# Hybrid attention and gated-unit layer on one core: finer jobs, one-operand VectorE forms, eight transposed-probability buffers, and a new hand-written order

## The chip, the cores and the metric

The kernel runs on one core of a Trainium2 chip. The metric is device time in microseconds (us), median of several runs. All engines of the core take part: TensorE (PE; its weight loads are PEld), VectorE (DVE), ScalarE (ACT), GpSimd (POOL) and SyncE (SP), which issues most DMAs.

## The reference

An input x of 8 blocks of 256 rows by 128 columns passes four stages, each added to x. LN is a LayerNorm with epsilon 1e-5.

```python
# A: attention without softmax, weights from a time difference
Q, K, V = sigmoid(4*(batchnorm(LN(x) @ W) - 1))           # for q, k, v
d = (1 - Q.mean(-1)) - (1 - K.mean(-1)).T                 # 256 x 256
x = x + (where(d < 0, f, -f) + 0.9) @ V @ Wo + bo         # f = 0.9*exp(-|d|/0.5)
# F: gated unit, hidden width 384, int weights / 127
x = x + (silu(LN(x) @ wg.T) * (LN(x) @ wu.T)) @ wd.T
# B: causal softmax attention, 16 heads of 64
x = x + attention(LN(x))
# P: the gated unit again, same weights as F
x = x + (silu(LN(x) @ wg.T) * (LN(x) @ wu.T)) @ wd.T
```

All is float32; products of float32 accuracy are built from a rounded high part (hi) and the rest (lo).

## The kernel before, in words

x stays in SBUF, with 128 rows to a partition dimension and two halves per block. Weights and x are loaded once at the start; block b's result is stored when dbP.b has been added.

There is no loop over the work. Each engine has a hand-written list of jobs, `ORDER`, and issues its jobs strictly in that order; a job is a name and a number, as `aout.3`. For the stages A, F and P and for projections of v the number is the block (0 to 7); for a pair of heads it is 8 x block + pair (0 to 63). Jobs meet by semaphores. The eight PSUM banks are shared by all: `BANKS` says which bank a job's result goes to, and `take` makes TensorE wait until the bank's last user has been read (`freed`), `full` makes a reader wait until TensorE has written. A change of an order therefore changes which job each bank waits for, too.

Jobs of one block, in the order in which they depend on each other:

- `lns` (VectorE: bn_stats, bn_aggr, then var = variance + epsilon, line 707; GpSimd: rstd by a power, line 863, and xn, line 874; in block 0 and for P.7 xn is on VectorE, line 717). The three come in one job of VectorE and one of GpSimd.
- `lnt` (TensorE transposes xn, ScalarE writes hi at line 576, VectorE lo at line 776). A, F, B and P at its end name the stage.
- Stage A: `qkv0..2` (TensorE, then tanh on ScalarE, line 587), `mean` (TensorE line 386, then VectorE: tq and ntk out of the bank, then less from tq, ntk and a zero mask, line 739), `dist` (ScalarE: |d| and exp), `sign` (VectorE line 795, both operands in SBUF), `stdp` (GpSimd line 909), `sv` (GpSimd), `vwo`, `aout` (TensorE line 404; VectorE adds to x, line 751; GpSimd's `lnsA` has put the bias in xb before).
- Stages F and P: `gF0..2` and `gP0..2`, one for each third of the hidden width (TensorE; ScalarE tanh; VectorE two operations, lines 787 and 788), then `hh` (ScalarE: hi of all three thirds in one instruction of 128x768, line 619), `hl` (GpSimd: lo, 128x768, line 903), `dn` (TensorE line 424, ScalarE), `db` (TensorE line 441 or 435, VectorE adds to x, line 755).
- Stage B, for each of 64 pairs: `qk` (TensorE; VectorE line 832 adds the bias), `scores` (TensorE lines 503 and 506), `mask` (VectorE lines 805 and 807: mask and row maximum; four instructions), `exp0`, `exp1` (ScalarE lines 645 and 647), `inverse` (VectorE line 822), `norm` (GpSimd line 916, two instructions of 128x256), `transposes` (TensorE line 518), `pt0` (ScalarE line 655) and `pt1` (VectorE line 815) into prob_t, and for two pairs at once `sum` (TensorE line 541, ScalarE). `v0..v3` give the values, `out0`, `out1` the projection (TensorE line 469, VectorE line 762); `pre0`, `pre1` start the last block's projection with six of eight pairs.
- `hot` is four transposes of the identity (lines 454 to 456) whose result nobody reads. `w0..w5` split the projection weights wqkv into hi (ScalarE line 611) and lo (GpSimd line 896, 128x512 each). `bo` adds a bias.

Buffers: three for qk, two for masked scores, four for prob, four for prob_t.

Of the kernel before, what the change touches and what calls it, by code (L numbers as in the profile page):

```python
# [39 lines left out]
W_SCALE = 1.0 / 127.0  # L40
SCORE_SCALE = A ** -0.5
# [12 lines left out]
        lntB.1 aout.2 lntA.3 v3.1 qk.8 qk.9 qk.10 qk.11 transposes.4 transposes.5 scores.8 scores.9 sum.5 transposes.6
        transposes.7 v2.1 v1.1 lntF.2 sum.7 scores.10 scores.11 gF1.2 qkv1.3 gF2.2 gF0.2 qk.12 qk.13 out0.0 v0.1 transposes.8
        transposes.9 scores.12 scores.13 out1.0 dnF.2 qkv2.3 qk.14 qk.15 qkv0.3 dbF.2 sum.9 transposes.10 transposes.11
        transposes.12 transposes.13 mean.3 vwo.3 lntB.2 scores.14 scores.15 sum.11 v3.2 lntP.0 qk.16 qk.17 aout.3 v2.2 scores.16
        scores.17 sum.13 qk.18 lntF.3 gP2.0 qk.19 v0.2 v1.2 transposes.14 transposes.15 scores.18 scores.19 transposes.16 sum.15
        transposes.17 gF1.3 gF0.3 gF2.3 qk.20 qk.21 lntA.4 qk.22 out1.1 scores.20 scores.21 gP0.0 gP1.0 out0.1 dnF.3 qkv1.4
        qkv0.4 qkv2.4 dbF.3 sum.17 transposes.18 scores.22 transposes.19 mean.4 qk.23 lntB.3 sum.19 transposes.20 transposes.21  # L60
        qk.24 qk.25 lntP.1 vwo.4 scores.23 scores.24 scores.25 qk.26 v0.3 gP2.1 lntA.5 aout.4 sum.21 transposes.22 transposes.23
        qk.27 gP0.1 dnP.0 qk.28 scores.26 scores.27 transposes.24 lntF.4 qkv2.5 v2.3 qk.29 v1.3 qkv1.5 gF0.4 gP1.1 gF1.4 gF2.4
        qkv0.5 scores.28 transposes.25 sum.23 sum.25 qk.30 qk.31 dnF.4 out0.2 dbF.4 mean.5 transposes.26 scores.29 transposes.27
        out1.2 lntB.4 vwo.5 v3.3 scores.30 scores.31 aout.5 qk.32 qk.33 dbP.0 lntP.2 dnP.1 v2.4 sum.27 transposes.28
        transposes.29 scores.32 scores.33 transposes.30 v1.4 lntA.6 lntF.5 qk.34 qk.35 dbP.1 gF1.5 gF2.5 v0.4 sum.29 scores.34
        scores.35 transposes.31 gF0.5 qkv0.6 qkv1.6 qk.36 qk.37 sum.31 transposes.32 transposes.33 gP2.2 out0.3 v3.4 dnF.5
        scores.36 scores.37 qkv2.6 dbF.5 gP0.2 qk.38 qk.39 vwo.6 mean.6 gP1.2 out1.3 lntB.5 transposes.34 transposes.35 sum.33
        sum.35 scores.38 scores.39 transposes.36 transposes.37 qk.40 qk.41 aout.6 dnP.2 v2.5 scores.40 scores.41 lntP.3 qk.42
        v1.5 v0.5 gP0.3 qk.43 lntF.6 sum.37 transposes.38 transposes.39 gF0.6 dbP.2 gF1.6 gF2.6 sum.39 scores.42 scores.43
        transposes.40 transposes.41 lntA.7 qk.44 qk.45 dnF.6 out0.4 qkv1.7 dbF.6 qkv2.7 qkv0.7 scores.44 scores.45 gP2.3 qk.46  # L70
        mean.7 lntB.6 gP1.3 out1.4 qk.47 vwo.7 sum.41 transposes.42 transposes.43 transposes.44 scores.46 scores.47
        transposes.45 sum.43 lntP.4 qk.48 qk.49 qk.50 dnP.3 aout.7 v3.5 scores.48 scores.49 transposes.46 sum.45 transposes.47
        v2.6 gP1.4 qk.51 lntF.7 gP2.4 dbP.3 gP0.4 sum.47 scores.50 scores.51 gF0.7 v1.6 gF2.7 qk.52 qk.53 gF1.7 out1.5 out0.5
        transposes.48 transposes.49 scores.52 scores.53 transposes.50 v0.6 dnF.7 qk.54 qk.55 dnP.4 dbF.7 transposes.51 scores.54
        scores.55 sum.49 sum.51 lntB.7 dbP.4 v3.6 lntP.5 qk.56 qk.57 qk.58 v2.7 transposes.52 transposes.53 scores.56 scores.57
        transposes.54 gP0.5 qk.59 qk.60 transposes.55 scores.58 scores.59 sum.53 sum.55 gP2.5 v0.7 out1.6 qk.61 v1.7
        transposes.56 transposes.57 scores.60 scores.61 transposes.58 qk.62 qk.63 out0.6 v3.7 scores.62 transposes.59 scores.63
        transposes.60 transposes.61 sum.57 lntP.6 gP1.5 sum.59 sum.61 transposes.62 transposes.63 pre0.0 gP2.6 gP1.6 sum.63
# [880 lines left out]
```

## Time and profile before

| what | value |
|---|---|
| median of 3 runs | 334.7 us (333.91 to 335.21) |
| the profiled execution's own time | 336.41 us |
| its span, first to last instruction | 334.6 us |
| granted TensorE clock | 0.998 |
| PE, PEld | 316.2, 272.4 us |
| DVE, ACT, POOL | 271.7, 245.3, 225.6 us |

The span is 1.8 us shorter than the profiled execution's time. Times of the views are counted from the span's start. Matmuls are pipelined: the durations of single matmuls overlap, so one matmul's step is better seen in the chain, where overlapping pieces are counted once.

### The profile page before, as it was taken

To read this page: it belongs to the slowest core of one execution; us is meant where nothing else is said; L and a number is where in the kernel's file an instruction comes from. 1 tells how busy PE (TensorE), PEld (TensorE's weight loads), DVE (VectorE), ACT (ScalarE), POOL (GpSimd) and SP (SyncE) were. 2 spreads that over 40 slices of the span, in tenths; PEclk is the share of its full clock that TensorE was granted. 3 is DMA by queue.
4 is the path that set the end of the run, shared out by engine and by line. 5 is a ranking of instruction groups with operands and counts; after the bars stand their busy time and mean duration, and the time that the engine had idled before them with its cause. 6 is when DMAs were issued, how large, how long until landed. Compare 5 with 4: busy or idle time off the path is not lost.

```text
span 334.6 us, 9995 instructions
## 1 busy us (share of the span) xinstructions
PE 316.2 (95%) x3216; PEld 272.4 (81%) x3216; DVE 271.7 (81%) x1092; ACT 245.3 (73%) x812; POOL 225.6 (67%) x279
## 2 busy tenths in 40 slices
PE   1998998999999999999999999999999999999995
PEld 1788886879978987898878887889888988888874
DVE  4547899868799999988998879978997988879454
ACT  2626497988779777887777876977967786698821
POOL 4437986747868879656889476863993398457630
PEclk9999999999999999999999999999999999999999
DMA  6900000000000000000001000000000000000001
GB/s 189 306 1 3 2 2 3 2 1 3 2 0 4 2 2 1 3 2 3 0 9 29 2 1 3 0 18 3 3 2 5 14 2 17 4 2 3 2 0 49
DMA packets 6419, 5.84 MB, mean 17 GB/s; under 512 B 864, under 2 KB 5856, under 8 KB 6368
## 3 DMA queue, kind: packets, MB, share of 16 engines
q1 hardware_dynamic: 6080, 4.99, 5.0%
q8 instruction: 27, 0.44, 0.5%
q10 hardware_dynamic: 288, 0.20, 0.2%
q14 instruction: 24, 0.20, 0.2%
HBM read 4.15 MB, written 1.05 MB: 16 GB/s over the span
## 4 chain that ended last, share of the span: by engine, by line
PE 77%; DVE 8%; issue 6%; POOL 4%; ACT 2%; DMA 1%; DVEq 0%; ACTq 0%; POOLq 0%
PE bank L541 12%; PE bank L355 8%; PE bank L518 7%; PE bank L506 7%; PE bank L357 6%; PE bank L356 6%; PE bank L469 6%; PE bank L503 5%; PE bank L415 4%; PE bank L416 3%; PE bank L424 2%; PE bank L373 2%; PE bank L404 2%; POOL prob L916 1%; PE bank L396 1%
## 5 line engine op out<-in xcount | busy, mean ns | idle before, releaser
L916 POOL TENSOR_TENSOR prob<-prob,row_inv 128x256 f32<-128x256 f32 (+1 forms) x128 | 103.0, 832 | 50.0 <-DVE row_inv L822 49.7
L647 ACT ACTIVATE prob<-neg_s,neg_max 128x256 f32<-128x256 f32 x128 | 63.9, 499 | 0.0
L645 ACT ACTIVATE prob<-neg_s,neg_max 128x128 f32<-128x128 f32 x128 | 50.8, 397 | 13.1 <-DVE neg_max L807 12.8
L807 DVE CUSTOM_DVE_ANT_0 neg_s<-bank,mask 128x256 f32<-128x256 f32 x128 | 53.5, 418 | 0.0
L541 PE MATMUL bank<-prob_t,v 128*64 128x256 f32 (+1 forms) x512 | 47.4, 331 | 0.0
L832 DVE TENSOR_TENSOR qk<-bank,bqk 128x512 f32<-128x512 f32 x64 | 42.7, 683 | 3.9 <-PE bank L357 3.7
L541 PEld LDWEIGHTS bank<-prob_t,v 128*64 128x64 f32 x512 | 32.1, 136 | 13.6 <-issue 2.9
L805 DVE CUSTOM_DVE_ANT_0 neg_s<-bank,mask 128x128 f32<-128x128 f32 x128 | 36.3, 284 | 4.6 <-PE bank L506 4.3
L506 PE MATMUL bank<-qk 64*128 64x256 f32 x256 | 38.5, 377 | 0.0
L355 PE MATMUL bank<-rt_hi,wqkv_hi 128*128 128x256 f32 x128 | 38.1, 298 | 0.4 <-DVE rt_lo L776 0.4
L815 DVE COPY prob_t<-bank 128x384 f32<-128x384 f32 x64 | 33.4, 548 | 4.3 <-PE bank L518 4.1
L518 PEld LDWEIGHTS bank<-ident,prob 64*128 64x128 f32 x768 | 28.9, 139 | 8.8 <-issue 4.9
L357 PE MATMUL bank<-rt_lo,wqkv_hi 128*128 128x256 f32 x128 | 35.8, 280 | 0.0
L356 PE MATMUL bank<-rt_hi,wqkv_lo 128*128 128x256 f32 x128 | 35.8, 280 | 0.0
L655 ACT ACTIVATE prob_t<-bank 128x384 f32<-128x384 f32 x64 | 29.3, 485 | 8.6 <-PE bank L518 8.4
L518 PE MATMUL bank<-ident,prob 64*128 64x64 f32 x768 | 32.7, 226 | 1.8 <-DVE qk L832 0.8
L469 PE MATMUL bank<-wo,zt 128*128 128x128 f32 x232 | 28.4, 276 | 0.0
L503 PE MATMUL bank<-qk 64*128 64x128 f32 x256 | 27.9, 295 | 0.0
L469 PEld LDWEIGHTS bank<-wo,zt 128*128 128x128 f32 x232 | 27.1, 192 | 0.5 <-issue 0.3
L503 PEld LDWEIGHTS bank<-qk 64*128 64x128 f32 x256 | 21.8, 187 | 6.4 <-issue 3.1
L355 PEld LDWEIGHTS bank<-rt_hi,wqkv_hi 128*128 128x128 f32 x128 | 24.1, 188 | 2.2 <-issue 0.8
L645 ACT ACTIVATION_READ_ACCUMULATOR prob<-neg_s,neg_max 128x1 f32 x128 | 24.8, 193 | 0.0
(162 smaller groups left out, 831.1 us busy)
## 6 DMA issues: line engine op xcount, KB each, us to landing
wqkv<-wqkv_in SPq DMA_DIRECT2D x3, 512.0 KB, 7.4
x<-x_in SPq DMA_DIRECT2D x8, 128.0 KB, 6.0
out<-x SPq DMA_DIRECT2D x8, 128.0 KB, 1.8
wo<-wo_in SPq DMA_DIRECT2D x1, 512.0 KB, 7.0
wa<-wa_in ACTq DMA_DIRECT2D x1, 192.0 KB, 3.0
wg_i<-wg_in SPq DMA_DIRECT2D x1, 192.0 KB, 3.2
wu_i<-wu_in SPq DMA_DIRECT2D x1, 192.0 KB, 3.4
wd_i<-wd_in SPq DMA_DIRECT2D x1, 192.0 KB, 4.4
```

The costliest lines, as they stand in the source:

```text
L355: nc.tensor.matmul(out, w_hi_ap, r_hi_ap, start=True, stop=False)
L356: nc.tensor.matmul(out, w_lo_ap, r_hi_ap, start=False, stop=False)
L357: return nc.tensor.matmul(out, w_hi_ap, r_lo_ap, start=False, stop=True)
L469: last = nc.tensor.matmul(out[:, 0:D], zt[:, b % 2, u, j * P:(j + 1) * P], wo[:, u, :], start=(u == 0), stop=(u == U - 1))
L503: nc.tensor.matmul(home(f"s{e}", m)[0][:, 0:P], qk[half, r, 0, 0:P], qk[half, r, 1, 0:P], start=True, stop=True)
L506: nc.tensor.matmul(S[:, P:SC], qk[half, r, 0, P:N], qk[half, r, 1, :], start=True, stop=True).then_inc(done, 1)
L518: last = nc.tensor.transpose(out[:, at:at + A], prob[half, m % 4, e, j * P:(j + 1) * P], ident[half, half])
L541: last = nc.tensor.matmul(out[half, t + k * P:t + N], v[:, b % 2, k, h * A:(h + 1) * A], prob_t[:, i % 4, e, cols], start=(k == 0), stop=( ...
L645: nc.scalar.activation(prob[:, r, e, 0:P], neg_s[:, m % 2, e, 0:P], ACT.Exp, bias=neg_max[:, q, 2 * e:2 * e + 1], scale=-1.0, accum_out=ro ...
L647: nc.scalar.activation(prob[:, r, e, P:SC], neg_s[:, m % 2, e, P:SC], ACT.Exp, bias=neg_max[:, q, 2 * e + 1:2 * e + 2], scale=-1.0, accum_ ...
L807: nc.vector.tensor_tensor_reduce(out=neg_s[:, m % 2, e, P:SC], in0=S[:, P:SC], in1=mask[:], scale=-SCORE_SCALE, scalar=3e38, op0=ALU.add, ...
L916: nc.gpsimd.tensor_tensor(pr, pr, inv, ALU.mult).then_inc(p_norm, 1)
```

## The change

1. *Epsilon.* bn_aggr now writes to `mv_eps`, three numbers per half: mean, variance and a constant EPS set once by a memset. var is a tensor_reduce that adds the last two.
2. *Comparison from PSUM.* ntk = -(k + 0.5) becomes tk = k + 0.5, and less is a tensor_scalar that reads the bank and compares with tk; the bank is freed after it. dist waits for a semaphore of its own, mean_s, and is abs(tk - tq) by a scale of -1.
3. *Gated units by chunk.* hh and hl become three jobs each, of 128x256.
4. *Eight buffers of prob_t*, four of them in the space of wqkv, which is read for the last time when all six weight parts are split.
5. *Finer jobs.* What VectorE's and GpSimd's first `lnsA` held of the A stage's constants becomes `ga` and `gb`, the VectorE xn becomes `xnA.0`, `xnF.0`, `xnB.0`, `xnP.7`, the casts of the gated unit's weights `wf`, the bias of stage A `xb`. Three of the six lo parts of wqkv (`w0`, `w2`, `w4`) are VectorE's.
6. *New lists and banks* for all engines; 18 `hot` jobs, 16 before.

```diff
-        last = nc.vector.bn_aggr(mv[c][:, j, :], stats[c][:, j, :])
+        last = nc.vector.bn_aggr(mv[c][:, j, 0:2], stats[c][:, j, :])
     link(last)
-    nc.vector.scalar_tensor_tensor(var[c][:], mv[c][:, :, 1], EPS, mv[c][:, :, 1], ALU.add, ALU.max).then_inc(var_s[k], 1)
+    nc.vector.tensor_reduce(out=var[c][:], in_=mv[c][:, :, 1:3], axis=mybir.AxisListType.X, op=ALU.add).then_inc(var_s[k], 1)
...
     nc.vector.tensor_scalar(tq[:, b % 2, :], src[:, 0:N], 0.5, None, ALU.add)
-    nc.vector.tensor_scalar(ntk[:, b % 2, :], src[:, N:N + T], 0.5, -1.0, ALU.add, ALU.mult).then_inc(free, 1)
+    nc.vector.tensor_scalar(tk[:, b % 2, :], src[:, N:N + T], 0.5, None, ALU.add).then_inc(mean_s, 1)
...
     for j in range(T):
-        last = nc.vector.scalar_tensor_tensor(less[:, j, :].rearrange("p (k s) -> p k s", s=P), tq[:, b % 2, :].rearrange("p (k s) -> p k s", s=P),
-                                              ntk[:, b % 2, j:j + 1], mask[:, 0:P].unsqueeze(1).to_broadcast([P, T, P]), ALU.add, ALU.is_lt)
-    last.then_inc(less_s, 1)
+        last = nc.vector.tensor_scalar(less[:, j, :], src[:, 0:N], 0.5, tk[:, b % 2, j:j + 1], ALU.add, ALU.is_lt)
+    last.then_inc(free, 1)
...
-    nc.scalar.activation(hid_hi[k][:], hid[k][:], ACT.Copy).then_inc(hh_s[k], 1)
+    nc.scalar.activation(hid_hi[k][:, c, :], hid[k][:, c, :], ACT.Copy).then_inc(hh_s[k][c], 1)
...
-    nc.gpsimd.tensor_tensor(hid_lo[k][:], hid[k][:], hid_hi[k][:].bitcast(F32), ALU.subtract).then_inc(hl_s[k], 1)
+    nc.gpsimd.tensor_tensor(hid_lo[k][:, c, :], hid[k][:, c, :], hid_hi[k][:, c, :].bitcast(F32), ALU.subtract).then_inc(hl_s[k][c], 1)
...
+elif job[0] == "w":                       # VectorE: w0, w2, w4
+    i = int(job[1])
+    dve.wait_ge(w_hi[i], 1)
+    ws = slice(i % 2 * HALF, (i % 2 + 1) * HALF)
+    nc.vector.tensor_tensor(wqkv_lo[:, i // 2, ws], wqkv[:, i // 2, ws], wqkv_hi[:, i // 2, ws].bitcast(F32), ALU.subtract).then_inc(w_lo[i], 1)
...
+def weights_split(eng, m):                # called by both evacuations into prob_t
+    if m == PT_BUFS // 2:
+        for i in range(6):
+            eng.wait_ge(w_lo[i], 1)
```

The start of the lists, as far as the prediction speaks of it:

```diff
 PE
-lntA.0 hot.0 qkv1.0 qkv0.0 qkv2.0 mean.0 vwo.0 lntA.1 hot.1 hot.2 hot.3 qkv0.1 aout.0 qkv1.1 hot.4 hot.5 mean.1 qkv2.1
-lntF.0 hot.6 hot.7 gF2.0 gF0.0 gF1.0 bo.0 lntA.2 dbF.0 qkv2.2 vwo.1 hot.8 qkv1.2 qkv0.2 hot.9 lntB.0 aout.1 qk.0 qk.1
+hot.0 hot.1 hot.2 hot.3 hot.4 lntA.0 hot.5 qkv0.0 qkv1.0 qkv2.0 mean.0 lntA.1 hot.6 hot.7 qkv0.1 qkv1.1 vwo.0 hot.8
+aout.0 mean.1 hot.9 hot.10 lntF.0 qkv2.1 hot.11 gF0.0 gF2.0 gF1.0 lntA.2 bo.0 dbF.0 qkv2.2 hot.12 vwo.1 vwo.2 qkv0.2
+qkv1.2 lntB.0 aout.1 qk.0 qk.1 v3.0 scores.0 scores.1
...
+lntB.1 aout.2 lntA.3 qk.8 qk.9
 DVE
-lnsA.0 lntA.0 lnsA.1 mean.0 sign.0 lntA.1 lnsA.2 aout.0 lnsF.0 bv.0 lntF.0 mean.1 gF2.0 gF0.0 gF1.0 lntA.2 sign.1 dbF.0
-lnsB.0 lnsA.3 lntB.0 bo.0 aout.1
+lnsA.0 ga.0 xnA.0 lnsA.1 lntA.0 gb.0 mean.0 lntA.1 sign.0 wf.0 w4.0 aout.0 lnsF.0 lnsA.2 xnF.0 mean.1 lntF.0 bv.0 gF0.0
+gF2.0 gF1.0 w2.0 lntA.2 sign.1 bo.0 dbF.0 lnsB.0 w0.0 xnB.0 lnsA.3 lntB.0 aout.1
 ACT
-lntA.0 qkv1.0 qkv0.0 qkv2.0 w3.0 w2.0 dist.0 lntA.1 w4.0 vwo.0 qkv0.1 qkv1.1 qkv2.1
+lntA.0 qkv0.0 qkv1.0 w0.0 qkv2.0 lntA.1 dist.0 w4.0 vwo.0 qkv0.1 w3.0 qkv1.1
```

and their end:

```diff
 PE
-... sum.59 sum.61 transposes.62 transposes.63 pre0.0 gP2.6 gP1.6 sum.63
-gP0.6 pre1.0 out0.7 out1.7 dnP.5 hot.10 hot.11 hot.12 lntP.7 hot.13 hot.14 gP2.7 gP0.7 gP1.7 dbP.5 dnP.6 hot.15 dbP.6 dbP.7
+... transposes.61 transposes.62 transposes.63 sum.61 sum.63
+lntP.6 pre0.0 gP2.6 out0.7 pre1.0 out1.7 gP1.6 dnP.5 gP0.6 hot.13 hot.14 lntP.7 hot.15 hot.16 gP2.7 gP0.7 gP1.7 dnP.6
+dbP.5 hot.17 dbP.6 dbP.7
 DVE
-lntP.6 gP1.5 pt1.62 pt1.63 gP2.6 gP1.6 gP0.6 out0.7 out1.7 lnsP.7 lntP.7 gP2.7 gP0.7 gP1.7 dbP.5 dbP.6 dbP.7
+lntP.6 out0.7 gP2.6 out1.7 lnsP.7 gP1.6 xnP.7 gP0.6 lntP.7 gP2.7 gP0.7 gP1.7 dbP.5 dbP.6 dbP.7
```

## Rows read from the trace of the kernel before

**Rows 1.** The page: busy time of each engine, its share of the span, instructions.
```profile
PE 316.2 (95%) x3216; PEld 272.4 (81%) x3216; DVE 271.7 (81%) x1092; ACT 245.3 (73%) x812; POOL 225.6 (67%) x279
```

**Rows 2.** Chain that ended last, 0 to 36 us: start us, us, what.
```profile
10.84 1.22 PE bank L386 x2
...
12.07 0.65 PE bank L388 x4
...
18.58 1.29 PE bank L404 x8
...
28.91 1.31 DVE signed L795
...
34.74 0.39 PE bank L355
```

**Rows 3.** Timeline, 14 to 36 us: start us, us, instruction [idle before <-releaser].
```profile
15.74 0.62 POOL L909 TENSOR_SCALAR stdp<-signed 128x512 f32<-128x512 f32 x1 [2.85 <-DVE signed L795]
...
19.90 0.42 DVE L751 TENSOR_TENSOR x<-bank,xb 128x256 f32<-128x256 f32 x1 [3.05 <-PE bank L404]
...
21.44 0.60 PE L386 MATMUL bank<-t_qkv,mean_w 128*128 128x256 f32 x2
...
24.03 1.96 POOL L874 TENSOR_SCALAR xn_A<-x,mv_A,rstd_A 128x128 f32<-128x128 f32 x2
...
24.60 0.89 DVE L739 SCALAR_TENSOR_TENSOR less<-tq,ntk,mask 128x256 f32<-128x256 f32 x2
...
30.58 0.49 DVE L700 BATCH_NORM_STATS2 stats_B<-x 128x6 f32<-128x128 f32 x2
```

**Rows 4.** Timeline around the longest hole on TensorE, 48 to 53 us.
```profile
48.32 2.87 DVE L739 SCALAR_TENSOR_TENSOR less<-tq,ntk,mask 128x256 f32<-128x256 f32 x2
...
48.89 2.01 POOL L903 TENSOR_TENSOR hid_lo_F<-hid_F,hid_hi_F 128x768 fp32r<-128x768 f32 x1
...
52.44 0.59 PE L424 MATMUL bank<-hid_hi_F,wd 128*128 128x256 f32 x3 [1.54 <-DVE neg_max L807]
```

**Rows 5.** Timeline, three more holes on TensorE (129 to 276 us).
```profile
131.44 0.59 PE L518 MATMUL bank<-ident,prob 64*128 64x64 f32 x12 [0.77 <-DVE qk L832]
...
208.68 0.53 PE L518 MATMUL bank<-ident,prob 64*128 64x64 f32 x10 [0.56 <-issue]
...
275.27 0.41 PE L441 MATMUL bank<-ident,dnt_F 128*128 128x128 f32 x2 [0.45 <-DVE qk L832]
```

**Rows 6.** Costs by line: instruction xcount | busy us, mean ns | idle before.
```profile
L707 DVE SCALAR_TENSOR_TENSOR var_P<-mv_P 128x2 f32<-128x2 f32 x7 | 4.4, 634 | 0.2
...
L707 DVE SCALAR_TENSOR_TENSOR var_A<-mv_A 128x2 f32<-128x2 f32 x8 | 3.1, 382 | 0.3
...
L739 DVE SCALAR_TENSOR_TENSOR less<-tq,ntk,mask 128x256 f32<-128x256 f32 x16 | 10.7, 711 | 0.3
...
L733 DVE TENSOR_SCALAR tq<-bank 128x256 f32<-128x256 f32 x8 | 3.3, 414 | 3.5 <-PE bank L388 3.5
...
L896 POOL TENSOR_TENSOR wqkv_lo<-wqkv,wqkv_hi 128x512 fp32r<-128x512 f32 x6 | 7.6, 1282 | 0.7 <-DVE xn_B L717 0.7
...
L619 ACT ACTIVATE hid_hi_F<-hid_F 128x768 fp32r<-128x768 f32 x7 | 5.9, 848 | 2.5 <-DVE hid_F L788 2.4
...
L903 POOL TENSOR_TENSOR hid_lo_F<-hid_F,hid_hi_F 128x768 fp32r<-128x768 f32 x7 | 13.0, 1856 | 4.9 <-ACT hid_hi_F L619 4.9
...
L744 DVE CAST wg<-wg_i 128x384 fp32r<-128x384 int32 x1 | 0.4, 353 | 0.0
```

**Rows 7.** Line 707: duration ns min/median/max, first and last start.
```profile
L707 DVE SCALAR_TENSOR_TENSOR var_P<-mv_P x7: 161/775/953, 92.7 to 306.0; 128x2 f32<-128x2 f32 x7
```

**Rows 8.** Chain that ended last, 320 to 326 us: start us, us, what.
```profile
320.40 0.89 PE bank L469 x8
...
324.19 0.45 PE bank L373 x2
...
325.55 0.39 PE bank L415
```

More of the change, by code:

```diff
@@ L54 @@
[L54 to L78, printed above, removed]
@@ new lines @@
+        aout.3 lntP.0 v3.2 scores.16 scores.17 sum.13 qk.18 qk.19 lntF.3 gP2.0 v2.2 v1.2 v0.2 transposes.14 transposes.15
+        scores.18 scores.19 transposes.16 transposes.17 sum.15 gF1.3 gP1.0 gF2.3 gF0.3 lntA.5 qkv2.4 out1.1 qk.20 qkv0.4 qk.21
+        qk.22 scores.20 scores.21 dnF.3 out0.1 dbF.3 gP0.0 transposes.18 scores.22 transposes.19 sum.17 qkv1.4 qk.23 lntB.3
+        vwo.4 mean.4 qk.24 qk.25 sum.19 transposes.20 transposes.21 scores.23 scores.24 scores.25 sum.21 qkv2.5 aout.4 lntP.1
@@ new lines @@
+        v0.3 qk.26 qk.27 gP2.1 dnP.0 transposes.22 transposes.23 scores.26 scores.27 transposes.24 v1.3 lntF.4 qk.28 qk.29
+        lntA.6 qk.30 qkv1.5 gF1.4 gP1.1 qkv0.5 gF0.4 gF2.4 v2.3 vwo.5 gP0.1 qk.31 scores.28 transposes.25 sum.23 sum.25 dbP.0
+        dnF.4 mean.5 dbF.4 out1.2 transposes.26 transposes.27 scores.29 scores.30 scores.31 out0.2 lntB.4 aout.5 dnP.1 v2.4
+        qk.32 qk.33 v3.3 qkv2.6 sum.27 transposes.28 transposes.29 scores.32 scores.33 transposes.30 lntF.5 v0.4 qk.34 v1.4
@@ new lines @@
+        gF1.5 qkv1.6 qk.35 gF0.5 gF2.5 scores.34 scores.35 transposes.31 sum.29 qk.36 vwo.6 qk.37 lntP.2 dbP.1 transposes.32
+        scores.36 scores.37 transposes.33 sum.31 gP1.2 gP2.2 dnF.5 out1.3 dbF.5 qkv0.6 qk.38 v3.4 qk.39 mean.6 gP0.2 out0.3
+        lntB.5 lntA.7 transposes.34 transposes.35 sum.33 sum.35 transposes.36 scores.38 scores.39 transposes.37 qk.40 aout.6
+        v0.5 v2.5 lntP.3 qk.41 qkv2.7 scores.40 scores.41 qkv0.7 gP0.3 lntF.6 dnP.2 v1.5 qk.42 dbP.2 gF2.6 qk.43 gF1.6 gF0.6
@@ L81 @@
+        scores.63 transposes.59 transposes.60 gP1.5 v3.7 sum.57 sum.59 transposes.61 transposes.62 transposes.63 sum.61 sum.63
+        lntP.6 pre0.0 gP2.6 out0.7 pre1.0 out1.7 gP1.6 dnP.5 gP0.6 hot.13 hot.14 lntP.7 hot.15 hot.16 gP2.7 gP0.7 gP1.7 dnP.6
+        dbP.5 hot.17 dbP.6 dbP.7
     """,
     "ACT": """
[L83 to L84 removed]
```

390 lines of the change are left out of this document (208 added, 182 removed).

## The prediction

> **What bounds the kernel now.** I read the page's first part, the chain of waits of the start, the timeline of the start, the costs by line, and last the timeline around the holes on TensorE. TensorE has work for 316.2 us, 95% of the span, VectorE 81% [rows 1]. From about 35 us on TensorE is the bound, and VectorE is the engine that hands it its banks. So time can come from three places: the start, where a serial chain runs until qk.0 begins at 34.74 us [rows 2]; the holes between 35 and 320 us; and the end, where the last block runs alone.
>
> The start is slow for two reasons. TensorE works at 1.2 GHz at first: mean.0 takes 1.22 + 0.65 us on the chain [rows 2], while the two matmul records of the same line L386 in mean.1 take 0.60 us at 21.44 [rows 3]. The granted clock of the run is 0.998, which hides it, so the level has to be read from the durations; the halving lies inside aout.0, which started in a nearly unbroken run of transposes. And aout.0 runs late: stdp.0 is written by 15.74 + 0.62 = 16.36 us, but aout.0's work ends on the chain at 18.58 + 1.29 = 19.87 us, and the x of block 0 is there at 19.90 + 0.42 = 20.32 us [rows 2, 3].
>
> The holes have one author. A VectorE instruction with two SBUF inputs does not run while GpSimd runs a tensor operation: less at 48.32 takes 2.87 us for two instructions while GpSimd's 768-wide hid_lo runs from 48.89 to 50.90, mask stands behind it in VectorE's order, and TensorE waits 1.54 us for that mask's bank [rows 4]. The others are 0.77, 0.56 and 0.45 us, behind less or var in the same way [rows 5]. The sum is 3.3 us. The same in the costs by line: var_P takes 634 ns for 128x2, var_A 382 ns, less 711 ns against 414 ns of tq, which reads one operand from PSUM [rows 6].
>
> **The change part by part.**
>
> *Start, up to x of block 0.* Five hot jobs (20 transposes) stand ahead of lntA.0. They need ident alone, ready near 2 us, and at a cold step of about 0.21 us end near 6.4 us, just before the first LayerNorm result (lntA.0 began at 6.68 us; it isn't held up). TensorE should then be at 2.4 GHz well before 19 us; I take before 9 us. VectorE runs lnsA.1 (about 1 us, half of it the two statistics, as in stats_B [rows 3]) before lntA.0, but the four small gb operations behind it, so qkv0.0 can start near 8.1 us; t_qkv waits for gb until about 9.35 us. mean.0 then starts near 10.5 (10.84 before) and takes 0.8 us in place of 1.87 [rows 2], ending near 11.3 us. From mean.0's end to stdp.0's took 16.36 - 12.72 = 3.6 us [rows 2, 3]; with lntA.1 put in on both ScalarE and VectorE I take 4.1, so stdp.0 is there at about 15.4 us. wf.0 and w4.0 (three casts of 0.35 and 0.8 us) now stand between sign.0 and aout.0 on VectorE and cover the 0.9 us of the matmuls with some to spare: x of block 0 near 16.8 us, 3.5 us earlier. At a still cold TensorE the gain is 1.5 us, and if aout.0 were to wait for vwo.0, which stands behind w4's copy on ScalarE, 3.0.
>
> *Start, from there to qk.0.* Before, this took 34.74 - 20.32 = 14.4 us. Three things are added on VectorE: mean.1 goes between xnF.0 and lntF.0 (1.4 us in a gap of 1.0: +0.5); w2.0 and bo.0 go ahead of dbF.0 beside sign.1, which took 1.31 us there [rows 2] (+0.4); w0.0 fills the wait for rstd_B. The last is the place where a rule speaks against the change. What the trace shows: GpSimd is held up by VectorE too; its two xn_A operations at 24.03 take 1.96 us beside less at 24.60 [rows 3]. So w0.0, issued directly behind var_B, holds rstd_B up: its cost on VectorE lies between 2 x 0.414 = 0.83 (twice tq) and 1.28 us (the same work on GpSimd, L896) [rows 6]; I take 0.83, of which 0.6 is delay. Removed: 0.2 us of lnsA.3's var. Together 14.4 + 1.3 = 15.7 us, and qk.0 starts near 32.5 us. Gain of the start: 2.2 us (bounds 0 and 4).
> The Trainium skill (SBUF — State Buffer, section "Who interferes with whom") has this as a lock on a shared port pair: a VectorE instruction with two SBUF inputs against a GpSimd one that reads SBUF, with issue order deciding who blocks, and tensor_reduce never contending. By that rule, the trace agrees at both places cited; without it for w0.0 the sum would be 0.6 us smaller.
>
> *Epsilon by tensor_reduce.* All 32 var operations were scalar_tensor_tensor on mv, twice read; now one operand is read. The trace has no tensor_reduce; I bound it by 0.16 us (the smallest var [rows 7]) and 0.6 (var_P's mean [rows 6]), and take 0.17, since it is as small an access. VectorE is relieved of (634 - 165) x 7 + (382 - 165) x 8 = 5.0 us in P and A alone [rows 6], and the LayerNorm that waits for it too. The one memset of EPS at the start lies under the first x load.
>
> *less from PSUM.* 16 x (711 - 414) = 4.8 us off VectorE [rows 6], and it holds nobody up. The mean bank is freed by the last less, some 0.8 us later than by ntk; it costs nothing where the bank's next user is over 2 us away, 0.2 us in one or two blocks. dist now waits for mean_s at the same point as before.
>
> *Gated units by chunk.* hid_hi was 848 ns once and becomes three of 128x256: between 0.28 (a third) and 0.41 us each (as tq); hid_lo was 1856 ns and becomes three of 0.62 to 0.8 [rows 6]. ScalarE gets 14 x 0.3 = 4 us more work and GpSimd about as much; both idle over a quarter of the span [rows 1], so 0 on the end. In return VectorE can be held up 0.7 us at once, not 1.8, and dn is ready about 1.5 us earlier.
>
> *Eight prob_t buffers, split of w, bo, xb, xn jobs.* No row shows an evacuation into prob_t waiting for a sum, so the buffers bring 0 by themselves (bounds 0 and -1). Their wait for all six w_lo comes at transposes.4, some 25 us after the last of these.
>
> *New orders, 35 to 320 us.* The four holes (3.3 us) come from var and less behind a long GpSimd operation, and both causes go. Against that, new places are tight: lntB.1 aout.2 lntA.3 qk.8 leaves 0.9 + 0.2 = 1.1 us, where the way from transposes to the next matmul took 325.55 - 324.19 - 0.22 = 1.14 us with free engines [rows 8]; there are four such blocks for two before, qk.41 and qk.45 have their scores 1.1 us behind, and dbF follows dnF at 0.7 to 0.8 in three blocks. I put 1.1 us on them (bounds 0 and 4). Net gain 2.2 us; vwo.2, now done in the start, is another 0.4.
>
> *End.* Between out1.7 and lntP.7 TensorE had 320.40 + 0.89 = 321.29 to 324.19 us [rows 8], filled with dnP.5 (0.7 us) and hot jobs. Now gP1.6 and gP0.6 (0.92 us) stand in there too, and xnP.7 stands after gP1.6 on VectorE, which the wait for rstd covers to within 0.1. What stays behind sum.63 is shorter; I take 1.0 us (bounds 0.3 and 1.3). The rest to the last store keeps its length.
>
> **Sum.** 2.2 + 2.2 + 0.4 + 1.0 = 5.8 us. Against the profiled execution (336.4 us, a span of 334.6 and 1.8 around it) that is 330.6; the median of the runs was 334.7, so 328.9 us.
>
> **Rivals.**
> 1. *The warm-up doesn't take.* TensorE stays at 1.2 GHz until aout.0 as before: 2 us less gained on x of block 0, 0.3 made good later. For it: the halving came late although TensorE had worked through mean.0 and most of what follows. Against: the new run is unbroken from 2 to 6.4 us. 330.6 us.
> 2. *The holes are only moved.* TensorE's order has new tight places, and VectorE is 81% busy; what var and less give back is taken by waits of 0.1 to 0.3 us at other banks. Start and end alone remain: 334.7 - 3.6 = 331.1 us. Against: every hole of 0.4 us and more lay behind one of the two operations.
> 3. *Relief spreads.* VectorE loses some 10 us of work, banks come free earlier everywhere, and gaps too short to be seen as waits shrink as well; half of the 10 us shows. 334.7 - 10 = 324.7 us.
> 4. *Slower: evacuation of qk becomes the gate.* scores.m needs qk.m out of its bank. Where VectorE has a mask pair in front (2 x 0.4 us and more) and the distance is 1.1 to 1.5 us, TensorE waits. With 64 of them, a wait of 0.12 us at each is 8 us and outdoes the 5.8: 334.7 - 5.8 + 8 = 336.9 us. It decides from 0.09 us each. For it: the three closest distances fell from 1.4 to 1.1 us. Against: most lie over 2 us.
>
> **How the numbers follow.** The forecast 328.9 has 0.45 (its own range 326.8 to 330.2), rival 1 0.14, rival 2 0.21, rival 3 0.13, rival 4 0.07. The range 324.8 to 332.5 leaves about 0.15 out. Faster by over 0.5% (1.7 us, about what a measurement can tell from no change) is below 333.0: all but rival 4 and a bad edge of rival 2, 0.89; same 0.06; slower 0.05.
>
> **What would show it.** L386 in mean.0 at 0.6 us and not 1.2; x of block 0 near 16.8 us, qk.0 near 32.5; rstd_B starting or lasting 0.6 us longer beside w0.0; every var near 0.17 us and every less near 0.41 with one long GpSimd operation in sight; no TensorE wait above 0.5 us between 35 and 320 us; from out1.7 to lntP.7 still about 3 us. It is wrong if var or less are still stretched, if mean.0 still takes 1.9 us, or if TensorE's waits in the middle sum to over 4 us.

## The result, and the profile after

The changed kernel took 322.53 us (median of 4 runs, 322.44 to 323.62), the kernel before 334.35 (333.91 to 335.21) beside it: a ratio of 0.965 (95% interval 0.962 to 0.968), 11.8 us less. The forecast was 328.9 us with a range of 324.8 to 332.5: the sign was right, the size half of what came.

The profiled execution of the changed kernel took 322.44 us with a span of 320.7, against 336.41 and 334.6 before, so the two traces differ by 13.9 us, 2 us more than the medians. The first part of the page after answers to [rows 1]: 5.7 us less work on TensorE and 8.4 us less on VectorE in a span 13.9 us shorter.

```profile
PE 310.5 (97%) x3224; PEld 272.9 (85%) x3224; DVE 263.3 (82%) x1096; ACT 247.4 (77%) x840; POOL 227.2 (71%) x304
```

The costs by line after (columns as in [rows 6]):

```profile
L772 DVE TENSOR_SCALAR less<-bank,tk 128x256 f32<-128x256 f32 x16 | 7.0, 480 | 0.3
...
L640 ACT ACTIVATE hid_hi_F<-hid_F 128x256 fp32r<-128x256 f32 x21 | 8.5, 418 | 3.6 <-DVE hid_F L815 3.5
...
L932 POOL TENSOR_TENSOR hid_lo_F<-hid_F,hid_hi_F 128x256 fp32r<-128x256 f32 x21 | 15.0, 734 | 7.3 <-ACT hid_hi_F L640 7.2
```

The line of var after, against 161/775/953 in [rows 7], and that of less (duration in ns, min/median/max):

```profile
L730 DVE TENSOR_REDUCE var_A<-mv_eps x8: 156/157/158, 5.0 to 184.6; 128x2 f32<-128x4 f32 x8
...
L730 DVE TENSOR_REDUCE var_P<-mv_eps x7: 157/158/158, 88.0 to 298.2; 128x2 f32<-128x4 f32 x7
...
L772 DVE TENSOR_SCALAR less<-bank,tk x16: 474/480/485, 11.7 to 225.2; 128x256 f32<-128x256 f32 x16
```

Each takes the same time to within 11 ns wherever it stands: no GpSimd operation stretches them any more. The start, in the chain that ended last (as [rows 2]; L407 is mean.0):

```profile
10.15 0.67 PE bank L407 x2
```

and in the timeline (as [rows 3]); L754 and L755 are two of wf.0's casts, L760 at 15.79 is w4.0, L778 writes the x of block 0, 0.41 us long, and the last row is qk.0:

```profile
14.20 0.66 POOL L938 TENSOR_SCALAR stdp<-signed 128x512 f32<-128x512 f32 x1 [2.37 <-DVE signed L822]
14.29 0.78 DVE L754 CAST wu<-wu_i 128x384 fp32r<-128x384 int32 x1
...
14.99 0.88 DVE L755 CAST wd<-wd_i 128x384 fp32r<-128x384 int32 x1
...
15.79 0.68 DVE L760 TENSOR_TENSOR wqkv_lo<-early,wqkv_hi 128x512 fp32r<-128x512 f32 x1
...
16.39 0.41 DVE L778 TENSOR_TENSOR x<-bank,xb 128x256 f32<-128x256 f32 x1
...
27.65 0.68 DVE L760 TENSOR_TENSOR wqkv_lo<-early,wqkv_hi 128x512 fp32r<-128x512 f32 x1
27.82 1.09 POOL L891 TENSOR_TENSOR rstd_B<-var_B,minus_half 128x2 f32<-128x2 f32 x1
...
31.06 0.36 PE L376 MATMUL bank<-rt_hi,wqkv_hi 128*128 128x256 f32 x1
```

The waits of TensorE over the whole run (engine, line, what it waited for, us, times, longest); this view lists what is idle beyond the modelled ends of matmuls:

```profile
PE bank L476 <- POOL ident L880: 2.0, 1, 2.0
PE bank L407 <- ACT t_qkv L609: 0.9, 2, 0.6
PE bank L394 <- DVE xn_F L736: 0.6, 1, 0.6
```

The larger ones all lie in the start. Nothing answers to [rows 4, 5]: where TensorE waited 1.54, 0.77, 0.56 and 0.45 us, the longest wait left is 0.31 us (aout.2, at 55.25 us). The end, to be read beside [rows 8] (the chain; the first line closes out1.7, the second is lntP.7):

```profile
307.92 0.45 PE bank L491 x4
...
311.25 0.45 PE bank L394 x2
```

From 308.37 to 311.25 there are again 2.9 us, now with gP1.6 and gP0.6 inside.

**Where 13.9 us went.** Marks are starts of matmuls, found by laying TensorE's records against its list of jobs. qk.0 starts at 31.06 (before 34.74): 3.7 us. From there to the end of out1.7: 277.3 us (before 286.6): 9.3 us. From there to the end of the span 12.3 us (before 13.3): 1.0. Forecast were 2.2, 2.6 and 1.0; the last of these included the 0.9 us of gP1.6 and gP0.6 that left the middle, so the middle to compare with 2.6 is 8.3, and the end 1.9.

For the middle I use one more number. For each kind of job and kind of job behind it (scores behind qk, for instance) I take the distance from start to start that 15% of such pairs in all 20 profiles stay under, as a floor, and call the rest **waits**. It is a yardstick, not a view: how finely the kinds are divided moves the waits of both kernels together by a few us (to 16.4 and 9.2 us with every job name a kind of its own), their difference by 0.2 us. Between qk.0 and out1.7 the kernel before has 18.2 us of waits over a floor of 267.7; the changed one 10.8 over 265.9. So 7.4 of the 9.3 us are waits, and 1.9 less floor (0.9 is gP1.6 and gP0.6, 0.4 vwo.2, 0.5 other neighbours). By size: pauses of 0.25 us and more were 11 with 6.6 us together and are 2 with 0.8; smaller ones went from 11.5 to 9.9 us. The four holes of [rows 4, 5] are 4.1 of the 6.6 us by this measure, where the views name 3.3; the other seven, 0.26 to 0.52 us each, were named nowhere in the prediction. Of the 1.0 us at the end, all lies behind the last add of VectorE, which is over at 331.33 us before and at 318.40 after: 3.3 and 2.3 us to the end of the span.

### The profile page after: what moved, and what is told of

It reads as the page before. It is cut to its first block, busy times and chain, and to the rows that moved or that the text cites. A ratio compares the mean times of both kernels' runs of the same rounds, so it can differ in the third digit from the quotient of the medians.

```text
span 320.7 us, 10121 instructions
## 1 busy us (share of the span) xinstructions
PE 310.5 (97%) x3224; PEld 272.9 (85%) x3224; DVE 263.3 (82%) x1096; ACT 247.4 (77%) x840; POOL 227.2 (71%) x304
## 4 chain that ended last, share of the span: by engine, by line
PE 89%; DVE 4%; issue 2%; POOL 2%; ACT 1%; DMA 1%; POOLq 0%; DVEq 0%
PE bank L563 14%; PE bank L528 9%; PE bank L376 9%; PE bank L540 8%; PE bank L491 8%; PE bank L377 8%; PE bank L378 8%; PE bank L525 6%; PE bank L436 4%; PE bank L437 3%; PE bank L446 3%; PE bank L394 3%; PE bank L425 2%; PE bank L407 1%; DMA x<-x_in 1%
## 5 line engine op out<-in xcount | busy, mean ns | idle before, releaser
L540 PE MATMUL bank<-ident,prob 64*128 64x64 f32 x768 | 31.5, 225 | 0.0
L685 ACT ACTIVATE zt<-bank 128x512 f32<-128x512 f32 x32 | 19.1, 595 | 10.1 <-PE bank L563 10.1
L665 ACT ACTIVATION_READ_ACCUMULATOR prob<-neg_s,neg_max 128x1 f32 x128 | 24.8, 193 | 0.0
L667 ACT ACTIVATION_READ_ACCUMULATOR prob<-neg_s,neg_max 128x1 f32 x128 | 24.7, 193 | 0.0
L377 PEld LDWEIGHTS bank<-rt_hi,wqkv_lo 128*128 128x128 f32 x128 | 24.3, 190 | 0.5
L628 ACT ACTIVATE v<-bank 128x512 f32<-128x512 f32 x32 | 18.6, 594 | 7.5 <-PE bank L378 7.5
```

The lines of the kernel that those rows point to most:

```text
L377: nc.tensor.matmul(out, w_lo_ap, r_hi_ap, start=False, stop=False)
L540: last = nc.tensor.transpose(out[:, at:at + A], prob[half, m % PROB_BUFS, e, j * P:(j + 1) * P], ident[half, half])
L665: nc.scalar.activation(prob[:, r, e, 0:P], neg_s[:, m % SCORE_BUFS, e, 0:P], ACT.Exp, bias=neg_max[:, q, 2 * e:2 * e + 1], scale=-1.0, acc ...
L667: nc.scalar.activation(prob[:, r, e, P:SC], neg_s[:, m % SCORE_BUFS, e, P:SC], ACT.Exp, bias=neg_max[:, q, 2 * e + 1:2 * e + 2], scale=-1. ...
```

## The experiments

All figures are medians. "Kernel before" is its median in the same set of runs (333.5 to 337.9 us in single runs). qk.0 and waits are of the profiled execution. In all runs of "before + forms" the time is 2.5 to 3.6 us longer than the span, in those of the hybrid (new start, old rest) with new banks 1.9 to 3.1, and 3.4 in one run of the hybrid with the old ones, against 1.7 to 1.9 in every run of the kernel before; what that is stays open. In five profiled executions the granted clock, once risen, was at half again for a part of the start, and their qk.0 comes later: after, again (12.2 to 15.6 us), old forms (13.0 to 16.4), 4 prob_t (12.9 to 16.3), before + 5 hot jobs (14.8 to 18.2), and before + forms, thirds, 5 hot jobs (12.8 to 19.6).

| kernel | us (range) | before | qk.0 | waits |
|---|---|---|---|---|
| before, again | 336.24, one run | 335.39 | 34.74 | 18.3 |
| before + forms | 333.16 (331.02 to 334.54) | 335.39 | 33.68 | 16.5 |
| before + 5 hot jobs | 334.22 (332.93 to 335.97) | 335.39 | 33.56 | 18.3 |
| before + forms, thirds, 5 hot jobs | 331.01 (329.46 to 332.35) | 335.28 | 34.20 | 15.7 |
| before, new banks | 330.95 (330.28 to 332.42) | 336.35 | 32.90 | 15.9 |
| before, banks of two hot jobs | 334.78 (333.88 to 336.64) | 335.29 | 32.88 | 18.3 |
| new start, old rest | 330.23 (330.04 to 332.65) | 335.21 | 31.03 | 16.5 |
| the same, new banks | 327.99 (327.33 to 328.76) | 336.35 | 30.98 | 13.9 |
| after, old forms | 328.47 (327.45 to 329.89) | 335.39 | 32.38 | 15.6 |
| after, old less | 326.73 (326.11 to 327.10) | 336.35 | 31.23 | 14.9 |
| after, whole hidden | 326.90 (326.63 to 327.30) | 335.28 | 31.33 | 14.4 |
| after, 4 prob_t | 324.49 (324.15 to 325.51) | 335.21 | 32.05 | 12.6 |
| after, cold start | 323.14 (322.95 to 325.30) | 335.28 | 33.55 | 10.7 |
| after, again | 322.61 (322.29 to 323.72) | 335.28 | 32.50 | 10.7 |
| after, exchange | 322.31 (322.08 to 323.03) | 335.21 | 30.73 | 10.8 |
| the same + 3 hot jobs | 322.94 (322.80 to 323.07) | 335.21 | 31.45 | 10.8 |
| exchange, new banks | 321.77 (321.48 to 321.96) | 336.35 | 30.75 | 10.3 |
| exchange, 3 hot jobs, new banks | 321.51 (321.26 to 322.12) | 335.29 | 31.40 | 10.2 |

**The two ends repeated.**

> The kernel before, unchanged, profiled a second time. The first profiled execution took 336.4 us, 2 us over the median of its runs, and its last store landed late. Theory 'noise in the profile': this one is at 334 to 335 us, with the same holes between 35 and 320 us. Rival 'the holes vary from run to run': TensorE's waits in the middle differ by over 1 us in sum.

> The changed kernel, unchanged, as the common measure for this set. Theory: 0.965 of the kernel before, 322.5 to 323.5 us, TensorE's waits between 31 and 300 us under 1.5 us in sum, as in its first profile.

The trace of the kernel before repeats itself: the same marks to 0.1 us and the same holes, at 0.9 us above the median as well. So the gain of the middle isn't noise. The changed kernel came back at 322.61 us, but its profiled execution (323.72) had qk.0 at 32.5: the granted clock was at half from 12.2 to 15.6 us. Of four timed runs of the changed kernel the three with a mean granted clock of 1.0 took 322.44 to 322.60, the one with 0.995 took 323.62: such a fall goes with 1.1 us, and the same kernel shows it in one execution and not in another.

**The forms of var and less, in the old order and undone in the new.**

```
- scalar_tensor_tensor(var[c], mv[c][:, :, 1], EPS, mv[c][:, :, 1], ALU.add, ALU.max)
+ tensor_reduce(out=var[c], in_=mv[c][:, :, 1:3], axis=X, op=ALU.add)
- scalar_tensor_tensor(less[:, j], tq, ntk[:, j], mask.., ALU.add, ALU.is_lt)
+ tensor_scalar(less[:, j], src[:, 0:N], 0.5, tk[:, j], ALU.add, ALU.is_lt)
```

> The kernel before, its lists and banks kept; only var by tensor_reduce and less from PSUM. Theory 'port' (the two forms were what stretched VectorE and made the holes in the middle): var near 0.16 us and less near 0.45 us everywhere, the four holes gone, 334.4 - 4 to 6 = 328.5 to 330.5 us. Rival 'orders' (the old lists were made for the old durations and the new lists bring the gain): 332.5 to 334.5 us.

> The changed kernel with var as scalar_tensor_tensor of two SBUF operands and less from tq, tk and the zero mask, all in SBUF; lists, banks and the place where the mean bank is freed kept. Theory 'port': holes come back behind var and less, 322.5 + 4 to 7 = 326.5 to 329.5 us. Rival 'orders': the new lists keep VectorE far enough ahead, 323 to 324.5 us.

> The changed kernel with less as it was before (two SBUF operands, locked out by GpSimd), and var in its new form. Both old forms together cost 5.9 us there. Theory A (less carries most of it, as the 2.9 us less in the hole at 48 us of the kernel before lets expect): 325.5 to 327.5 us. Theory B (var carries it, since xn and the transposes wait for var and nobody waits for less): 322.8 to 324 us.

The forms gave the kernel before 2.2 us (ratio 0.990, 0.985 to 0.995), which is in the range of the rival "orders" and short of the theory's: its four large holes go, as the theory had it, and five others come (0.5 to 1.0 us each, more on them below), so that its waits fall by 1.7 us only. By the span they are worth more: its median is 330.1 us in these runs and 333.6 in those of the kernel before, 3.5 us less, and the other 1.3 us are the unexplained time around the span. Taking them out of the changed one cost 5.9 us, though the instructions are the same. Both old forms fall in the range of the theory "port", and less alone is 4.2 of the 5.9 (theory A). A stretch of the changed kernel with the old less, in the timeline:

```profile
125.02 1.96 DVE L774 SCALAR_TENSOR_TENSOR less<-tq,tk,mask 128x256 f32<-128x256 f32 x2
...
125.79 1.77 POOL L935 TENSOR_TENSOR hid_lo_P<-hid_P,hid_hi_P 128x256 fp32r<-128x256 f32 x2
...
126.90 1.28 DVE L863 TENSOR_TENSOR qk<-bank,bqk 128x512 f32<-128x512 f32 x2
...
128.28 0.43 PE L540 MATMUL bank<-ident,prob 64*128 64x64 f32 x7 [1.03 <-issue]
```

Two less take 1.96 us beside GpSimd's thirds, qk stands behind them in VectorE's order, and transposes.20 waits 1.03 us, since its bank is the one that qk.25 leaves at 128.19 us. It is the mechanism of [rows 4] with other actors: the new order has no slack behind less, because it was laid out for 0.96.

**The hidden layer whole again.** hid_hi and hid_lo as one 128x768 instruction each, at the place of the last third.

```
- hhF1.3 ... hhF2.3 ... hhF0.3      - hlF1.3 hlF2.3 hlF0.3
+ hhF.3                             + hlF.3
```

> The changed kernel with hid_hi and hid_lo each in one instruction of 128x768, at the place of the last of the three jobs; all else kept. Theory 'port' (a GpSimd operation of 1.9 us holds up VectorE's remaining operations with two SBUF inputs, and dn comes later): 1 to 3 us slower than the changed kernel, 323.5 to 326 us. Rival 'chunks cost more than they bring': the same or up to 1 us faster, as ScalarE and GpSimd have 4 us less to do.

It cost 4.3 us, over the range of both theories, and 3.6 us of waits. The largest new one:

```profile
217.86 1.81 POOL L897 TENSOR_TENSOR hid_lo_F<-hid_F,hid_hi_F 128x768 fp32r<-128x768 f32 x1 [1.74 <-ACT hid_hi_F L605]
...
219.73 0.39 PE L410 MATMUL bank<-hid_hi_F,wd 128*128 128x256 f32 x1 [1.45 <-POOL hid_lo_F L897]
```

GpSimd sat idle 1.74 us until hid_hi was whole, and dnF.6 waited 1.45 us for it. So thirds matter for when dn is ready, and the order counts on it.

**Hot jobs in front.**

> The kernel before with five more hot jobs ahead of lntA.0 and nothing else. Theory 'clock' (half of the gain at the start is TensorE at 2.4 GHz before 9 us): mean.0 takes 0.8 us and not 1.9, x of block 0 1.5 to 2 us earlier, 332.5 to 333 us. Rival 'order of the start': the chain runs through VectorE and ScalarE, under 0.5 us gained, 334 us.

> The changed kernel without the five hot jobs ahead of lntA.0. Theory 'clock': mean.0 takes 1.9 us again and the halving comes after 15 us; x of block 0 is 1.5 to 2 us later and the end as well, 324 to 325 us. Rival 'clock comes anyway' (the denser new start warms TensorE by itself): under 0.7 us.

In the kernel before five hot jobs gave 1.2 us (ratio 0.995, 0.993 to 0.998); without them the changed one lost 0.5 at the median. In its profiled execution without them (324.75) mean.0 took 1.8 us and qk.0 came at 33.55, but most of its runs took 323.0 to 323.2: so most executions lose less by a cold start than this one. Neither experiment came out in the range of its theory "clock". The step "TensorE at 2.4 GHz before 9 us" held, by the steps of the transposes (0.21 us up to 6.1 us, 0.11 from 7.1 on, in the changed kernel), but the start doesn't always keep it. With the five hot jobs in the kernel before the granted clock was at half again from 14.8 to 18.2 us, and aout.0 (17.30 us, 1.37 us long) ran at the slow level after all; eleven of that kernel's 12 runs have a mean granted clock of 0.995 and one 0.990, where 12 of the 17 runs of the kernel before have 0.998 or more. So its 1.2 us are likely what is left after such a fall; one execution alone has a trace.

**Forms, thirds and hot jobs together in the old order.**

> The kernel before, its lists and banks kept, with the one-operand forms, hid_hi and hid_lo in thirds (the three jobs one behind the other where the one stood), and five hot jobs in front. Theory 'parts add up' (forms 3.4, hot 1.6, thirds 1 to 3 us): 334.4 - 6 to 8 = 326.5 to 328.5 us, and what is left to 322.5, 4 to 6 us, is the lists' and banks'. Rival 'thirds do nothing in old lists': 329 to 330 us.

331.0 us, slower than both theories had it. Of the 12.7 us between the two kernels in this set (335.28 and 322.61) 8.4 are still missing with all cheap instructions in place. They are the order, its table of banks and the buffers.

**The new start before the old rest.** The changed kernel's lists up to qk.0, the old lists and banks behind it.

> The changed kernel's code and its start on every engine, up to qk.0, but behind it the order and the banks of the kernel before (with the gated units in thirds, xb on GpSimd and eight buffers). The kernel before with the forms, the thirds and the five hot jobs took 331.0 us, the changed one 322.6; so 8.4 us lie in the start's order, the rest's order with its banks, and the buffers. Theory A (the new order of the middle itself is worth over half of it, in TensorE's small waits): this kernel takes 327.5 to 329.5 us, qk.0 starts near 31 us and the waits between qk.0 and out1.7, by my floor, stay near 15.5 us. Theory B (the start's order and the buffers carry it, and the middle's order only moves work): 323.5 to 325 us, with waits near 11 us.

qk.0 starts at 31.03 us as in the changed kernel, yet the time is 330.2: the start is worth little over the kernel with forms, thirds and five hot jobs (331.0), and 7.7 us lie behind qk.0. Theory B is out, and A went further than its range. The largest holes of this kernel show one cause that the prediction had priced at 0.2 us in one or two blocks (timeline at 197 to 198 us):

```profile
197.11 0.88 DVE L680 TENSOR_SCALAR less<-bank,tk 128x256 f32<-128x256 f32 x2
...
198.13 0.41 PE L302 MATMUL bank<-ident,xn_B 128*128 128x128 f32 x2 [0.47 <-DVE less L680]
```

The new less reads the bank of mean to its end, 1 us longer than ntk did, and the old table gives that bank at once to lntB.5 here, to scores.5 and scores.15 at two other places. Three of the six largest holes (at 45.6, 90.1 and 198.1 us, 2.0 us together) are this one, and the kernel before with the new forms has the same three (1.9 us).

**The table of banks made anew.** Each use of a bank gets the one that has been free longest in the profile; the jobs and their order stay. Uses that begin within 0.3 us of the release fall from 70 to 5 of 526 in the kernel before, from 65 to 6 in the changed one, by the times of the profile that the table was made from.

> The kernel before with another table of banks and nothing else: each use gets the bank that had been free longest in the profile of the kernel before. In that profile 70 of the 526 uses of a bank begin within 0.3 us of its release and 142 within 0.6; in the new table these are 5 and 26. Theory A (part of TensorE's small waits are waits for a bank that was released just before): the waits between qk.0 and out1.7, by my floor, fall from 17.4 us to 14 or less, and the time is 331 to 333 us. Theory B (TensorE waits for data and for its engines, not for banks; a release 0.1 us ahead is early enough): 334.5 to 336 us, as before.

> The kernel with the new start and the old order of the rest, which took 330.2 us, with the table of banks made anew in the same way. Three of its six largest holes (at 45.6, 90.1 and 198.1 us, 2.0 us together) end with less, which now releases the bank of mean 0.9 us later than ntk did, under a table that was made for the earlier release. Theory A (the table was the cost): these three holes go, and the time is 327.5 to 328.3 us. Theory A+ (all tight banks cost): under 327 us. Theory B (the order, not the table, makes the rest): scores and lntB wait for the next thing at the same place, and it stays at 329.5 to 330.5 us.

> The changed kernel with lnsA.3 and w0.0 exchanged, which took 322.3 us, and the table of banks made anew in the same way: 65 uses within 0.3 us of the release become 6. Theory A (tight banks cost in the new table as well): 320 to 321.5 us. Theory B (the new table is already fitted to its order; no TensorE wait of over 0.6 us is left between qk.0 and out1.7): 322.0 to 322.6 us.

The table alone gave the kernel before 5 us (ratio 0.985, 0.982 to 0.988), a little more than theory A's range. Of the 5.2 us between the two spans 2.4 are waits, less than theory A had; 1.8 lie ahead of qk.0 and 1.0 behind the last add, two places whose share in the medians is open (see the hot jobs' banks and the end below). The hybrid gained 2.2 us and its three holes behind less are gone (theory A); the changed kernel 0.5 (all six runs below every run of the one it is made from), between its two theories. So tight banks did cost, most of all where the order wasn't made for them. With fresh tables on both sides the old order of the rest still needs 328.0 us and the new one 321.8: 6.2 us are the order itself, 3.7 of them waits and 1.4 floor (0.9 of these gP1.6 and gP0.6, moved behind out1.7); in the rest are a fall of the clock near the end of the hybrid's profiled execution (half from 316.2 to 319.6 us) and its longer time around the span.

**Four prob_t buffers in place of eight.**

```
- QK_BUFS, SCORE_BUFS, PROB_BUFS, PT_BUFS = 3, 2, 4, 8
+ QK_BUFS, SCORE_BUFS, PROB_BUFS, PT_BUFS = 3, 2, 4, 4
```

> The changed kernel with four prob_t buffers in place of eight and nothing else. Prediction's theory (no evacuation waits for a sum): 322.6 us, within 0.5. Rival (the new order has transposes running ahead of their sums, as transposes.4 to .7 before sum.5, and with four buffers the evacuation of the fourth waits for a sum that stands behind it): 324.5 us or more, with the loss at sums and transposes.

It cost 1.9 us, with new holes of 1.0 us at transposes.62, 0.9 at transposes.13 and 0.4 at transposes.63, where the prediction had 0. The rival with transposes running ahead of their sums is right. "No row shows an evacuation waiting for a sum" was read from an order that had been written for four buffers.

**w0.0 beside rstd_B.**

```
- lnsB.0 w0.0 xnB.0 lnsA.3 lntB.0
+ lnsB.0 lnsA.3 xnB.0 w0.0 lntB.0
```

> The changed kernel with lnsA.3 and w0.0 exchanged on VectorE: w0.0 no longer stands between var_B and rstd_B but behind xn_B, and lnsA.3 fills the wait for rstd_B. Theory (VectorE's w0.0 with two SBUF inputs holds GpSimd's rstd_B up by 0.4 us, on the path to qk.0): rstd_B takes 0.72 us in place of 1.09, qk.0 starts 0.3 to 0.4 us earlier, and the time is 322.2 us. Rival (w0.0 now meets GpSimd's w3.0 and waits for 1.2 us in front of lntB.0): rstd_B is short all the same, but qk.0 comes as late or later, 322.6 to 323.4 us.

As forecast: qk.0 0.33 us earlier, 322.31 us. The timeline of this kernel:

```profile
27.86 0.72 POOL L891 TENSOR_TENSOR rstd_B<-var_B,minus_half 128x2 f32<-128x2 f32 x1
...
30.73 0.35 PE L376 MATMUL bank<-rt_hi,wqkv_hi 128*128 128x256 f32 x1
```

rstd_B takes 0.72 us where it took 1.09 beside w0.0, while the one-input instructions of lnsA.3 now run beside it. The prediction put 0.6 us on this; it is 0.37. By the Trainium skill (SBUF — State Buffer, section "Who interferes with whom") a VectorE instruction with two SBUF inputs contends with a GpSimd instruction that reads SBUF, and issue order decides who waits. The trace agrees in direction: w0.0, issued 0.17 us ahead, had 0.51 us still to run, and rstd_B was 0.37 us longer.

**Hot jobs and their banks.**

> The same exchange on VectorE, and three more hot jobs in TensorE's order, ahead of qkv0.0, mean.0 and lntF.0, where it idled 0.3 to 0.6 us. In one profiled execution of the changed kernel the granted clock fell to half from 12.2 to 15.6 us and qk.0 came 1.4 us later. Theory (the fall comes from the idle stretches behind the first hot jobs, and filling them prevents it): no fall in the profile, all times within 0.5 us of each other, median 322.0 us, 0.2 below the kernel with the exchange alone. Rival (the fall comes anyhow, or the added jobs hold up qkv0.0 and mean.0, each job 0.44 us at the fast step): 322.3 to 323.2 us.

> The kernel before with two digits of its table changed: hot.2 and hot.3 write banks 1 and 2, where all three hot jobs behind lntA.1 had bank 0. In the profile of the kernel before 0.36 us lie idle ahead of hot.2 and of hot.3, each of which waits for the last transpose of the job ahead of it in the same bank, and the clock rose at 19.3 us; with the whole table made anew there is no such gap, the clock rose at 16.3 us and qk.0 came 1.8 us earlier. Theory A (the gaps broke the run of transposes that raises the clock): qk.0 near 33 us, and the time 1.5 to 2 us under the kernel before. Theory B (the gain of the start has another source in the new table, and the clock rises when it does): qk.0 at 34.3 us or later, 0 to 0.7 us under the kernel before.

> The kernel with the exchange and the three more hot jobs, which took 322.9 us, with the table of banks made anew, which gives neighbouring hot jobs different banks. Each of the added jobs had taken the bank of the hot job before it, and waited for it. Theory A (that wait is what they cost): mean.0 starts at 10.3 us in place of 10.9, and the time is within 0.3 us of the same kernel without them, 321.8 us. Theory B (the added jobs themselves are in the way of qkv0.0 and mean.0): mean.0 at 10.7 us or later and a time of 322.3 to 322.6 us.

Three more hot jobs first lost 0.6 us, as the rival had it, with mean.0 at 10.86 instead of 10.2. A hot job that has the bank of the hot job ahead of it waits for that one's last transpose. In the kernel before this is to be seen behind lntA.1 (TensorE's timeline), first with the old banks:

```profile
15.04 0.42 PE L456 MATMUL bank<-ident 128*128 128x128 f32 x1
15.61 0.66 PE L454 MATMUL bank<-ident 128*128 128x128 f32 x2
```

then with the banks of two hot jobs changed:

```profile
14.99 0.42 PE L456 MATMUL bank<-ident 128*128 128x128 f32 x1
15.21 0.64 PE L454 MATMUL bank<-ident 128*128 128x128 f32 x2
```

The next pair of hot jobs repeats it (16.28 and 16.85 us; 15.85 and 16.06). The steps were 0.21 us, then idle for 0.36; without the gap the run of transposes is unbroken, the granted clock rises at 16.3 us in place of 19.3, and qk.0 starts 1.9 us earlier. In the medians that is 0.5 us and not told from nothing (ratio 0.999, 0.997 to 1.002): theory A holds in the trace and fails on the time. That the moment of the rise differs from run to run would explain it; only one execution of each kernel has a trace, so it isn't shown. In the last kernel, with neighbouring hot jobs in different banks, mean.0 starts at 10.24 us, and it takes 321.51 us, as theory A had it: the fastest kernel here, 0.959 of the kernel before (0.956 to 0.962). Its profiled execution (322.12) is the slowest of its six. It and the exchange with new banks (321.77) beat both kernels of the study; their difference from each other is within their ranges.

## Why the prediction was too small

- **Start, up to x of block 0.** Right: forecast 16.8 us, found 16.39 + 0.41 = 16.8, mean.0 at the fast level and at 10.15 us for 10.5 (1.01 us long for 0.8). The exact figure is luck: stdp.0 was there at 14.86 us and not at 15.4, and wf.0 with w4.0 took 2.36 us (14.03 to 16.39) for 1.85, as two casts took 0.78 and 0.88 us; the two errors cancel.
- **Start, from there to qk.0.** Forecast 15.7 us, found 31.06 - 16.80 = 14.3. The additions were overpriced: w0.0 0.37 us for 0.6; sign.1 took 0.68 us where the row behind the forecast had 1.31, as GpSimd was idle beside it (22.14 to 26.22 us); the rest, some 0.6 us, is mean.1, w2.0 and bo.0, which cost less than put down. Against the trace the start gave 3.7 us for 2.2. Some 2 us of the profiled execution of before lie over its median, and the two-bank experiment shows that 1.9 us of its late start hardly appear in medians; so the forecast start may well be right for the median. That part stays open to about 1.5 us.
- **Epsilon and less.** Durations right: 157 ns for 0.17, 480 for 414 (two for 0.88 us). Their effect was mis-stated: "it holds nobody up" is false for less, which alone is worth 4.2 us in the new order. The late release of the mean's bank, forecast at 0.2 us in one or two blocks, is 0.3 us in the changed kernel (scores.4, at 45.26 us, takes the bank that mean.2 left 0.09 us before); with the old table it was 2.0 us.
- **Gated units by chunk.** Durations right (418 and 734 ns). Priced at 0 on the end; undone it costs 4.3 us.
- **Eight buffers.** Forecast 0, bound -1; undone it costs 1.9 us.
- **New orders, 35 to 320 us: the step that failed.** It went: four holes of 3.3 us go, 1.1 us of new tight places come, net 2.2 us. By the same measure on both sides, 6.6 us of holes went and 0.8 came or stayed, which is 5.8; smaller waits gave 1.6 and better neighbours 0.5: 7.9 us. So 3.3 was half of what there was. The waits view and the chain name only idle time beyond the modelled ends of matmuls, which cut 0.8 us off the four holes and, of seven more of 2.5 us, showed two in part (0.34 and 0.22 us); with TensorE 95% busy [rows 1] I took what was named for all. The 1.1 us of new tight places was too high as well: aout.2 behind lntB.1, the case worked out there, is the largest wait left, but with 0.5 us it is one of two. The experiments say why all went at once: forms, thirds, buffers, table and order each bring back holes of 0.3 to 1.5 us when one of them is missing.
- **The end.** Forecast 1.0, found 1.9: gP1.6 and gP0.6 0.9 us as forecast, and 1.0 behind dbP.7, which I had held constant. It lies behind the last add of VectorE, where the last store stands, and it isn't explained further; the forms alone, in the old order, show the same shortening (330.8 - 328.1 = 2.7 us from dbP.7 to the end, where before has 3.7), as do five hot jobs alone (2.7), which don't touch the end. Only the two profiled executions of the kernel before and that with the banks of two hot jobs changed show the longer end. So it isn't the work at the end that changed; but it came in both executions of the kernel before, so it isn't shown to be chance either, and whether this 1.0 us belongs to the change stays open.

Of the rivals the third, relief that spreads to gaps not seen as waits, came nearest with 324.7 us and a chance of 0.13; and it is nearer in the number than in the mechanism: in it the gain was half of VectorE's 10 us of relief (8.4 by the page), in gaps too small to be seen as waits, while of the middle's 7.9 us 5.8 were pauses of 0.25 us and more and 1.6 smaller ones.

The parts undone one at a time cost 5.9, 4.3, 1.9 and 7.7 us, together 19.8 for a gain of 11.8: none has a worth of its own. In the old order the forms are worth 2.2, and forms, thirds and hot jobs 4.3. The thirds alone and eight buffers alone weren't tried there.
